# Queries times the state: one block of half-height matmuls ahead of the third gate/up piece, in place of four full-height matmuls on a block diagonal copy of the state

## What is computed

```
gate_in = concat[q, k, v];  ig, fg = gate_in @ igate_w.T + b, gate_in @ fgate_w.T + b
log_D   = cumulated forget gates (row) - cumulated forget gates (column) + ig, lower triangle
D       = exp(log_D - max(log_D));   C = (q @ k.T / sqrt(dh)) * D
h       = (C / normalizer) @ v;      x = x + layernorm(h) * norm_w
g, y    = fp4(layernorm(x)) @ fp4(w_gate).T, ... @ fp4(w_up).T
x       = x + fp4(silu(g) * y) @ fp4(w_down).T
```

## Time and profile before

| | |
|---|---|
| median of 3 runs | 1907.06 us |
| span of the profiled execution | 1901.7 us |
| PE busy | 1798.2 us, 95% |
| DVE, ACT, POOL busy | 1557.4, 1420.0, 1184.2 us |
| mean granted TensorE clock | 0.973 of full speed |

### The profile page before, as it was taken

The page is one execution under the profiler, slowest core; times in us unless marked ns, Lnnn a source line. Parts: engine busy times, 40 slices in busy tenths (PEclk is TensorE's granted clock), DMA queues, the critical chain, the costliest instruction groups (busy, mean ns, idle before and its releaser), DMA issues. The chain is left out here.

```text
span 1901.7 us, 37200 instructions
## 1 busy us (share of the span) xinstructions
PE 1798.2 (95%) x11577; PEld 1050.8 (55%) x11577; DVE 1557.4 (82%) x3213; ACT 1420.0 (75%) x2958; POOL 1184.2 (62%) x1189
## 2 busy tenths in 40 slices
PE   4567999999999999999999999999999999999997
PEld 3434555555555555565555555555555555555553
DVE  8987888888887788888878888788888888789993
ACT  7765877777777777777777777777787777776763
POOL 7865666566656666666666666656666665656652
PEclk9667999999999999999999999999999999999998
DMA  6344435444434444444444444434444543444322
GB/s 213 100 92 94 112 110 126 99 115 120 118 107 110 119 108 118 116 118 106 108 120 113 113 114 116 114 106 117 123 105 110 120 126 100 115 103 103 93 66 62
DMA packets 342116, 211.47 MB, mean 111 GB/s; under 512 B 275200, under 2 KB 281856, under 8 KB 341920
## 3 DMA queue, kind: packets, MB, share of 16 engines
q1 hardware_dynamic: 341920, 209.10, 42.6%
HBM read 125.93 MB, written 17.30 MB: 75 GB/s over the span
## 5 line engine op out<-in xcount | busy, mean ns | idle before, releaser
L481 PE MATMUL bank<-wgTh,xqT 128*128 128x512 f16 (+1 forms) x1536 | 557.5, 363 | 8.2 <-DMA xqT<-xqs 8.1
L481 PE MATMUL bank<-wuTh,xqT 128*128 128x512 f16 (+1 forms) x1536 | 556.9, 363 | 0.0
L1069 POOL TENSOR_TENSOR stage<-stage,hs 128x512 f32<-128x512 f32 (+1 forms) x192 | 190.4, 992 | 432.6 <-DVE stage L1277 432.6
L605 PE MATMUL bank<-wdTh,work 128*128 128x512 f16 x704 | 269.0, 382 | 12.6 <-DMA work<-stage 12.6
L481 PE MATMUL bank<-wgTl,xqT 128*128 128x512 f16 (+1 forms) x768 | 278.6, 363 | 0.0
L481 PE MATMUL bank<-wuTl,xqT 128*128 128x512 f16 (+1 forms) x768 | 278.6, 363 | 0.0
L606 PE MATMUL bank<-wdTl,work 128*128 128x512 f16 x704 | 267.6, 380 | 0.0
L607 PE MATMUL bank<-wdTh,work 128*128 128x512 f16 x704 | 267.6, 380 | 0.0
L1122 POOL TENSOR_TENSOR stage<-stage,hinv 128x512 f32<-128x512 f32 (+1 forms) x192 | 239.5, 1249 | 8.2 <-DVE hinv L1362 8.1
L481 PEld LDWEIGHTS bank<-wgTh,xqT 128*128 128x128 f16 x1536 | 157.3, 102 | 152.7 <-DMA xqT<-xqs 15.6
L481 PEld LDWEIGHTS bank<-wuTh,xqT 128*128 128x128 f16 x1536 | 163.9, 107 | 131.8 <-issue 2.1
(11 more groups left out here) (208 smaller groups left out, 3917.4 us busy)
## 6 DMA issues: line engine op xcount, KB each, us to landing
mb<-max_dram SPq DMA_DIRECT2D x64, 512.0 KB, 4.0
x<-in_x_dram SPq DMA_DIRECT2D x64, 256.0 KB, 2.8
cf<-in_ctx_dram SPq DMA_DIRECT2D x64, 256.0 KB, 3.6
cn<-in_ctx_dram SPq DMA_DIRECT2D x64, 256.0 KB, 3.7
wb<-warp_dram SPq DMA_DIRECT2D x128, 128.0 KB, 3.2
out_dram<-ob SPq DMA_DIRECT2D x64, 256.0 KB, 3.6
xb<-in_x_dram SPq DMA_DIRECT2D x60, 256.0 KB, 2.6
work<-stage SPq DMA_TRANSPOSE x192, 3.1
```

Of the source, the lines that this page charges most:

```text
L481: i = e.matmul(o[:, 0:width], x, w[:, c, n0:n0 + width], start=first and k < 2, stop=last and k >= 4)
L605: e.matmul(DOWN[:, :], hi, wdT[0][:, c0 + c, :], start=(c0 + c == 0), stop=False)
L1069: e.tensor_tensor(blocks(hx[:, n0:n0 + w]), blocks(hx[:, n0:n0 + w]), per_block(hs2[:, n0 // BLOCK:(n0 + w) // BLOCK]), ALU.mult).then_inc ...
```

## The change

The four matmuls with `Sbd` leave the riders. In their place a new step `pe_qS` multiplies each head's queries with its state directly: for each pair of heads, one matmul on the upper 64 rows of the array and one on the lower 64 rows, each 65 columns wide, eight matmuls in all. They stand as one block ahead of piece 2. The two row halves write to different banks, so `U` is laid out anew: even heads in R2, odd heads in R0. The block now holds the waits for the readers of `GP` and `G`, and for `xT`, `cols`, `xw`, the first half of `C`, the state itself, and the copies `uc` of the tile before. The eight riders with `D` stay, now in the first eight of the twelve places. `Sbd` and its two copies on ACT go, `dve_Sd` waits for the block instead (`qS`), and in `dve_start` the four `dve_Sd` move to stand right ahead of `dve_St`. ACT's copies from `U` write with a stride.

```
 U = [b[:, 0:HC * DA].rearrange("p (c r d) -> p c r d", r=2, d=DA) for b in (R2, R0)]      # before
 U = [b[:, 0:HC * DA].rearrange("p (c d) -> p c d", d=DA) for b in (R2, R0)]               # after
...
-                    if n == 2 and c >= 2 and t.has(2) and rider.live(NT):
+                    if n == 2 and c >= 2 and 6 * (c - 2) + k < 8 and t.has(2) and rider.live(NT):
                         pe_u_part(e, rider, 6 * (c - 2) + k)
...
+        def pe_qS(e, t):
+            later = t.back(-5)
+            if later.live(NT + 1) and later.slot % 4 == 0 and later.has(4):
+                e.wait_ge(S_["cols"], later.quads(4))
+            if later.live(NT):
+                e.wait_ge(S_["xT"], later.done())
+                if later.has(1):
+                    e.wait_ge(S_["gpart"], later.pairs() if later.slot % 2 == 1 else later.pairs(1))
+                if later.slot % 4 == 3:
+                    e.wait_ge(S_["gr"], later.quads_of(4, 3))
+            if t.at_start(0):
+                e.wait_ge(S_["zero"], 1)
+            if t.has(8):
+                e.wait_ge(S_["St"], t.done(8))
+            e.wait_ge(S_["xw"], t.done())
+            e.wait_ge(s_C[0], t.done())
+            if t.has(1):
+                e.wait_ge(s_uc[0], t.done(1))
+                e.wait_ge(s_uc[1], t.done(1))
+            for c in range(HC):
+                for par in range(2):
+                    r = slice(par * DH, (par + 1) * DH)
+                    i = e.matmul(U[par][:, c, :], xw[r, c, :], St[t.slot][r, c, :], start=(c == 0), stop=False)
+            i.then_inc(S_["qS"], 1)
...
-            c, j = divmod(k, 3)
-            o = U[c // 2][:, c % 2]
-            if j == 0:
-                return e.matmul(o.rearrange("p r d -> p (r d)"), xw[:, c, :], Sbd[:, c, :, :].rearrange("p r d -> p (r d)"),
-                                start=(c % 2 == 0), stop=False)
-            i = e.matmul(o[:, j - 1, :], D[:, j - 1, c, :], vc[t.parity][:, 2 * c + j - 1, :], start=False, stop=(c % 2 == 1 and j == 2))
-            return i.then_inc(S_["u"], 1) if k == 11 else i
+            c, par = divmod(k, 2)
+            i = e.matmul(U[par][:, c, :], D[:, par, c, :], vc[t.parity][:, 2 * c + par, :], start=False, stop=(c == HC - 1))
+            return i.then_inc(S_["u"], 1) if k == 7 else i
...
 pe_turn:
                 pe_gate_mm(e, t1)
                 pe_pick_mm(e, t1)
+            if t6.live(NT):
+                pe_qS(e, t6)
             if t8.live(NT):
                 pe_gu(e, t8, 2)
...
 act_turn: both act_Sbd steps are gone; act_uc:
-            e.copy(uc[:, HC * k:HC * (k + 1), :], U[k].rearrange("p c r d -> p (c r) d")).then_inc(s_uc[k], 1)
+            e.copy(uc[:, :, :].rearrange("p (c r) d -> p r c d", r=2)[:, k], U[k]).then_inc(s_uc[k], 1)
...
 dve_Sd:
-            e.wait_ge(s_Sbd[0], t.done())
-            e.wait_ge(s_Sbd[1], t.done())
+            e.wait_ge(S_["qS"], t.done())
```

More of the change, by code:

```diff
@@ L243, in mlstm_fp4_ffn @@
         WROW = bank[3][:, 0:P]
-        U = [b[:, 0:HC * DA].rearrange("p (c r d) -> p c r d", r=2, d=DA) for b in (R2, R0)]
+        U = [b[:, 0:HC * DA].rearrange("p (c d) -> p c d", d=DA) for b in (R2, R0)]
         ST = R1[:, 0:HC * DA].rearrange("p (c d) -> p c d", d=DA)
@@ L273, in mlstm_fp4_ffn @@
         s_gu, s_silu, s_h = ([S_[f"{k}{n}"] for n in range(NP)] for k in ("gu", "silu", "h"))
-        s_mask, s_C, s_uc, s_Sbd = ([sem(f"s_{k}{n}") for n in range(2)] for k in ("mask", "C", "uc", "Sbd"))
+        s_mask, s_C, s_uc = ([sem(f"s_{k}{n}") for n in range(2)] for k in ("mask", "C", "uc"))
         s_hx, s_hz, s_h_t, s_h_q, s_h_qs, s_h_hi = ([sem(f"s_{k}{n}") for n in range(NP)] for k in ("hx", "hz", "h_t", "h_q", "h_qs", "h_hi"))
@@ L550, in pe_pick_mm @@
                 i.then_inc(S_["pick_mm"], 1)
+        def pe_qS(e, t):
[22 more added lines that the diff above has]
+            i.then_inc(S_["qS"], 1)
         def pe_u_part(e, t, k):
-            later = t.back(-5)
             if k == 0:
[L556 to L563, removed]
-                e.wait_ge(s_Sbd[0], t.done())
-                e.wait_ge(s_Sbd[1], t.done())
-                e.wait_ge(S_["xw"], t.done())
                 e.wait_ge(S_["vc"], t.done())
@@ L569, in pe_u_part @@
                 e.wait_ge(s_C[1], t.done())
-            c, j = divmod(k, 3)
-            o = U[c // 2][:, c % 2]
-            if j == 0:
-                return e.matmul(o.rearrange("p r d -> p (r d)"), xw[:, c, :], Sbd[:, c, :, :].rearrange("p r d -> p (r d)"),
-                                start=(c % 2 == 0), stop=False)
-            i = e.matmul(o[:, j - 1, :], D[:, j - 1, c, :], vc[t.parity][:, 2 * c + j - 1, :], start=False, stop=(c % 2 == 1 and j == 2))
-            return i.then_inc(S_["u"], 1) if k == 11 else i
+            c, par = divmod(k, 2)
+            i = e.matmul(U[par][:, c, :], D[:, par, c, :], vc[t.parity][:, 2 * c + par, :], start=False, stop=(c == HC - 1))
+            return i.then_inc(S_["u"], 1) if k == 7 else i
         def pe_u(e, t):
-            for k in range(12):
+            pe_qS(e, t)
+            for k in range(8):
                 pe_u_part(e, t, k)
@@ L750, in act_silu @@
             e.activation(sl[:, n0:n0 + w], pair(t, n)[0][:, 0:w], ACT.Silu, scale=wfix[:, 0:1]).then_inc(s_silu[n], 1)
[L752 to L760, removed]
         def act_xz(e, t):
@@ L1167, in pool_zero @@
                 e.memset(St[i][:, :, :], 0.0)
-            e.memset(Sbd[:, :, :, :], 0.0)
             for i in range(2):
@@ L1668, in dve_start @@
             dve_w_am(e, 2, 2); dve_w_q(e, 1, 3); dve_w_lo(e, 0, 9); dve_w_t(e, 1, 4); dve_w_q(e, 1, 4); dve_w_t(e, 1, 5); dve_w_lo(e, 0, 10); dve_w_am(e, 2, 3)
-            dve_C(e, T[0], 1); dve_w_q(e, 1, 5); dve_w_am(e, 2, 4); dve_w_lo(e, 1, 0); dve_w_wi(e, 2, 0); dve_Sd(e, T[0]); dve_C(e, T[0], 0); dve_w_lo(e, 1, 1)
-            dve_w_t(e, 1, 6); dve_w_q(e, 1, 6); dve_w_t(e, 1, 7); dve_w_am(e, 2, 5); dve_w_q(e, 1, 7); dve_w_t(e, 1, 8); dve_St(e, T[0]); dve_w_lo(e, 1, 2)
-            dve_w_lo(e, 1, 3); dve_w_t(e, 1, 9); dve_mc(e, T[3]); dve_w_q(e, 1, 8); dve_w_lo(e, 1, 4); dve_w_q(e, 1, 9); dve_w_am(e, 2, 6); dve_w_lo(e, 1, 5)
+            dve_C(e, T[0], 1); dve_w_q(e, 1, 5); dve_w_am(e, 2, 4); dve_w_lo(e, 1, 0); dve_w_wi(e, 2, 0); dve_C(e, T[0], 0); dve_w_lo(e, 1, 1)
+            dve_w_t(e, 1, 6); dve_w_q(e, 1, 6); dve_w_t(e, 1, 7); dve_w_am(e, 2, 5); dve_w_q(e, 1, 7); dve_w_t(e, 1, 8); dve_w_lo(e, 1, 2)
+            dve_w_lo(e, 1, 3); dve_w_t(e, 1, 9); dve_mc(e, T[3]); dve_w_q(e, 1, 8); dve_w_lo(e, 1, 4); dve_w_q(e, 1, 9); dve_w_am(e, 2, 6); dve_w_lo(e, 1, 5); dve_Sd(e, T[0]); dve_St(e, T[0])
             dve_w_am(e, 2, 7); dve_w_am(e, 2, 8); dve_w_am(e, 2, 9); dve_nr_neg(e, T[0]); dve_w_am(e, 2, 10); dve_w_lo(e, 1, 6); dve_w_wm(e, 2); dve_nr(e, T[0])
@@ L1674, in dve_start @@
             dve_w_top(e, 2); dve_ve(e, T[0]); dve_w_lo(e, 1, 9); dve_w_pw(e, 2); dve_C(e, T[1], 1); dve_w_lo(e, 1, 10); dve_C(e, T[1], 0); dve_w_ws(e, 2)
-            dve_hn(e, T[0]); dve_x1(e, T[0]); dve_Sd(e, T[1]); dve_w_t(e, 2, 0); dve_w_t(e, 2, 1); dve_w_q(e, 2, 0); dve_w_q(e, 2, 1); dve_xam(e, T[0])
+            dve_hn(e, T[0]); dve_x1(e, T[0]); dve_w_t(e, 2, 0); dve_w_t(e, 2, 1); dve_w_q(e, 2, 0); dve_w_q(e, 2, 1); dve_xam(e, T[0])
             dve_w_t(e, 2, 2); dve_nr_neg(e, T[1]); dve_sd2(e, T[0]); dve_w_t(e, 2, 3); dve_xt(e, T[0]); dve_w_q(e, 2, 2); dve_xi(e, T[0]); dve_nr(e, T[1])
-            dve_St(e, T[1]); dve_xn(e, T[0]); dve_w_lo(e, 2, 0); dve_w_t(e, 2, 4); dve_x_t(e, T[0]); dve_nq(e, T[1]); dve_w_t(e, 2, 5); dve_x_q(e, T[0])
+            dve_Sd(e, T[1]); dve_St(e, T[1]); dve_xn(e, T[0]); dve_w_lo(e, 2, 0); dve_w_t(e, 2, 4); dve_x_t(e, T[0]); dve_nq(e, T[1]); dve_w_t(e, 2, 5); dve_x_q(e, T[0])
             dve_n2(e, T[1]); dve_xs(e, T[0]); dve_w_q(e, 2, 3); dve_vr(e, T[1]); dve_x_lo(e, T[0]); dve_ve(e, T[1]); dve_w_q(e, 2, 4); dve_C(e, T[2], 1)
@@ L1681, in dve_start @@
             dve_xt(e, T[1]); dve_w_lo(e, 2, 6); dve_w_q(e, 2, 7); dve_w_t(e, 2, 9); dve_w_q(e, 2, 8); dve_h(e, T[0], 0); dve_xi(e, T[1]); dve_w_q(e, 2, 9)
[L1682 removed]
+            dve_w_t(e, 2, 10); dve_w_q(e, 2, 10); dve_ham(e, T[0], 0); dve_xn(e, T[1]); dve_w_lo(e, 2, 7); dve_w_lo(e, 2, 8); dve_h(e, T[0], 1)
             dve_x_t(e, T[1]); dve_h(e, T[0], 2); dve_ham(e, T[0], 1); dve_ham(e, T[0], 2); dve_w_lo(e, 2, 9); dve_ht(e, T[0]); dve_x_q(e, T[1])
[L1684 removed]
+            dve_w_lo(e, 2, 10); dve_hinv(e, T[0]); dve_x_lo(e, T[1]); dve_hs(e, T[0]); dve_F(e, T[7]); dve_hm(e, T[0]); dve_Sd(e, T[2]); dve_St(e, T[2]); dve_h_t(e, T[0], 1)
             dve_hpw(e, T[0]); dve_a(e, T[7]); dve_nr_neg(e, T[2]); dve_M(e, T[7]); dve_nr(e, T[2]); dve_vr(e, T[2]); dve_nq(e, T[2]); dve_row3(e, T[7])
@@ L1690, in dve_start @@
             dve_x_q(e, T[2]); dve_ht(e, T[1]); dve_nr_neg(e, T[3]); dve_h_lo(e, T[0], 2); dve_nr(e, T[3]); dve_nq(e, T[3]); dve_vr(e, T[3]); dve_hm(e, T[1])
```

(2 more changed lines are left out.)

24 lines of the change are left out of this document (8 added, 16 removed).

## The result

After the change the median of four runs is 1967.16 us (1965.21 to 1971.28), against 1907.7 us (four runs) before: slower, with a ratio of 1.0319 and a 95% interval of 1.0306 to 1.0332. The direction was as forecast; the size was not. Forecast were +36.7 us and a range up to 1960 us; it became +59.5 us, or +66.6 us between the two profiled spans.

A forecast was written before the change was run, and what follows sets the result against it. PE was taken to bound the kernel; -53.4 (riders) + 66 (block) + 9.2 + 17.4 (waits) - 2.5 (entry) = +36.7 us on the 1901.7 us span, 1938.4, with the median 5.4 above: 1944 us, range 1920 to 1960.

The forecast's parts named there:

- What bounds the kernel: Steady-state turns: PE is busy throughout, so its time sets the kernel's; ACT's two dropped copies of 0.41 us gain nothing.
- The block against the riders: Loop's 60 turns on PE: riders removed save 0.89 us each (-53.4 us), the block adds 1.10 us each (+66 us).
- The rival of a cheap block: `pe_qS` block on PE: it streams more cheaply, 0.71 us or so, giving 1920 us; chance 13%.
- The waits: Ahead of piece 2: PE waits for R2, 0.66 us in 14 slot 1 turns (+9.2), 1.24 in 14 slot 3 turns (+17.4).
- One mark that I had set: Profile after: PE's list of waits should name `gpart` and `ig` for the block's waits, 27 us in all.
- Entry inside the wait, -2.5 us: Block's start in 28 turns with waits: its 0.09 us entry lies inside the wait, so 2.5 us are taken off.
- `dve_Sd` in slot 3, 0 us: DVE waits up to 1.8 us for the block; almost 4 us to spare, so 0 taken, 11 us as upper end.
- The four moved `dve_Sd` in the start ... 0, between -4 and +5.: Start: the moved steps and four blocks change little, as DVE's work is unchanged and PE idles for other reasons.
- The clock, 6%: Slot 3 turns: PE's waits of 0.59 and 1.24 us lower the clock, 35 us more, 1979 us; chance 6%.

The follow-up runs named there:

- experiment 6: experiment 4 plus three more blocks behind the first: the same again, 33 streamed columns, 64 weight columns; only its trace read: 0.90, 0.96 and 0.61 us.
- experiment 3: Kernel before with only PE's waits for cols, xT, gpart and gr moved from the first rider to the front of piece 2: 1939.74 us, ratio 1.0172.
- experiment 4: experiment 1 with the block moved into the middle of piece 2 and the loop's `dve_Sd` next to `dve_St`: 1920.44 us, ratio 1.0072.
- experiment 1: Changed kernel with SP's load of `wb` for tile 3 moved behind the transpose of xqs of tile 1: 1951.08 us, ratio 1.0226.
- experiment 2: Kernel before with only `dve_Sd` of tile 2 moved right ahead of `dve_St` of tile 2: 1919.89 us, ratio 1.0071.
- experiment 5: experiment 4 with the block split into four pairs, each where a rider with `Sbd` rode: 1959.43 us, ratio 1.0273.

## Why the prediction was off, step by step

- **What bounds the kernel.** Right. PE's time in a turn is the turn; ACT's 47 us less are worth nothing.
- **The block against the riders.** Right: 1.15 us against the 1.10 taken, so +0.26 us in a turn without gates, against 0.21. The reason taken for it, that 128-column loads set the pace, is shown by experiment 6. The rival of a cheap block falls.
- **The waits.** Right in place, number and size: 14 of 0.64 and 14 of 1.23 us, 26.3 against 26.6. One mark that I had set was wrong: the profile names "issue" for them, not `gpart` and `ig`. That they are these waits shows in experiment 3, which has the 14 longer ones with `ig` by name, and in experiment 4, where R2 has long been free and they are gone.
- **Entry inside the wait, -2.5 us.** Too simple. The profile counts idle time from the end of a row, and a matmul's successor starts before that. By starts, `pe_pick_mm` to what follows grows from 1029.67 - 1028.72 = 0.95 to 961.35 - 959.01 = 2.34 us, 1.39 more, and in slot 1 from 1083.70 - 1083.15 = 0.55 to 1017.13 - 1015.88 = 1.25, 0.70 more. With the block's 1.06 and less the riders' 0.89 that makes 1.56 and 0.87, the measured turns. I had 1.24 and 0.66 there, so 28 turns cost about 3 us more.
- **`dve_Sd` in slot 3, 0 us.** DVE waits for the block longer than I had thought: 30.5 us over 14 turns, 2.2 each, where I had up to 1.8. It costs PE nothing that can be seen: the turns of slot 3 are accounted for without it.
- **"The four moved `dve_Sd` in the start ... 0, between -4 and +5."** This is the step that failed. It cost 14 to 15 us (14.1 by the start of `pe_qk` of tile 4; 15.0 and 13.3 by experiments 1 and 2). I counted DVE's own work and PE's idle time, and did not ask who waits for the moved step. SP does, for its load of `wb`, and the trace of before shows that load at once behind its neighbour at 143.3 us, 6 us behind `dve_Sd` at 137.1. With it was queued all that PE's next work needs: four pairs of weight transposes and `xqT`.
- **The clock, 6%.** Second miss. I priced it as all 14 turns or none; it came in five, for about 10 us (they are 11.3 us over 30.79, of which about 1 us is short waits of PE for other things). The rows before had a wait of 0.59 us alone at full clock. That said nothing of 0.59 and 1.23 us within 3 us.

The sum by what was measured: the loop's 60 turns by their most frequent lengths 32 x 0.26 + 14 x 0.86 + 14 x 1.56 = 42.2, start 14.1, the single long turns, mostly the clock, about 10, together 66.3, against 66.6 between the spans. The forecast had 36.7 for the first and nothing for the other two. It also set the median 5.4 us above the profiled span, and after the change it lies 1.1 us below; that is why the miss is 23 us and not 30. Why the clock falls in some turns of slot 3 and not in others, whose rows look alike, the runs don't settle.

## What to carry to other kernels

A step that is moved on one engine is moved for every queue that waits for it: list its readers and the semaphore it raises, DMA queues first, and see what is queued behind each of them. Weights cut in half along the rows did not load faster here, so where loading sets the pace the two halves side by side only made up for twice as many matmuls; and each switch of the array's form was paid for, so one switch was cheaper than four. And a wait in the bounding engine's queue belongs behind work that is ready: moving the wait of `pe_pick_mm` there won 6 us.

## What the runs showed of the hardware

- Entering a run of half-height matmuls costs 0.09 us and leaving it 0.02 before an fp16 matmul, more before an fp32 one (0.28 us to the next start in place of 0.17). In experiment 6 the first load of a block stands 0.32 us behind the end of the load ahead of it, and the next load behind the block is not early either: across the switch weights aren't loaded ahead.
- A second block of 8 half-height matmuls behind the first takes 0.90 us, with 65 columns or (0.96, a change to 64-wide weights included) 33; with 64 weight columns it takes 0.61.
- Behind two waits of 0.59 and 1.23 us within 3 us the granted clock fell to 0.50 in 5 of 14 turns (4 of 14 in experiment 1, and 1 of 14 in experiment 3 with waits of 0.59 and 1.28 us). In the loop of the kernel before, and of experiments 4 and 5, where a wait of 0.59 us stands alone, it did not fall. In the longest turn it stayed down for more than 4 us (508 to 512 above; gate/up matmuls are 0.32 us apart until 513.17).
